# Edge counts from source ramps made on ScalarE beside VectorE's one-hots, with the first up-projection between the count batches

## The reference, cut to what matters

```python
e = jax.nn.leaky_relu(alpha_src[src] + alpha_dst[dst], NEG_SLOPE)
m = jax.ops.segment_max(e, dst, num_segments=n)
p = jnp.exp(e - m[dst])
denom = jax.ops.segment_sum(p, dst, num_segments=n)
out = jax.ops.segment_sum(h[src] * (p / denom[dst])[:, :, None], dst, num_segments=n)
```

## Time and profile before

| what | value |
|---|---|
| median of 3 runs | 1407.78 us (1406.85 to 1408.96) |
| the profiled execution's own time | 1407.49 us |
| its span, first to last instruction | 1405.7 us |
| TensorE busy | 1310.6 us, 93% |
| VectorE busy | 1004.6 us, 71% |
| ScalarE busy | 627.4 us, 45% |
| mean granted TensorE clock | 0.98 of 2.4 GHz |

### The profile page before, as it was taken

The page is one execution under the profiler, slowest core; times in us unless marked ns, Lnnn a source line. Parts: engine busy times, 40 slices in busy tenths (PEclk is TensorE's granted clock), DMA queues, the critical chain, the costliest instruction groups (busy, mean ns, idle before and its releaser), DMA issues.

```text
span 1405.7 us, 21373 instructions
## 1 busy us (share of the span) xinstructions
PE 1310.6 (93%) x7833; PEld 1149.2 (82%) x7833; DVE 1004.6 (71%) x1677; ACT 627.4 (45%) x795; POOL 217.0 (15%) x160
## 2 busy tenths in 40 slices
PE   5799999997899999997898999999999999999986
PEld 4499999974689999975777898898889888988875
DVE  7888888877797888875856765666566556656565
ACT  2256665644355666553434433433343334333431
POOL 0033444431024344431000000000000000002000
PEclk9999999998999999998999999999999999999988
DMA  9466556653256555653334454445444544543520
GB/s 346 147 202 198 164 164 180 213 134 93 91 196 199 180 164 164 192 160 113 113 111 152 163 198 170 149 166 199 158 149 177 195 149 149 188 177 134 177 69 23
DMA packets 103718, 227.32 MB, mean 162 GB/s; under 512 B 16688, under 2 KB 34672, under 8 KB 103684
## 3 DMA queue, kind: packets, MB, share of 16 engines
q1 hardware_dynamic: 72780, 192.43, 39.1%
q10 hardware_dynamic: 20968, 31.78, 7.7%
q0 software_dynamic: 9936, 2.66, 1.9%
HBM read 216.56 MB, written 10.29 MB: 161 GB/s over the span
## 4 chain that ended last, share of the span: by engine, by line
PE 61%; DVE 24%; issue 8%; ACT 4%; DMA 1%; DVEq 1%; ACTq 0%; SPq 0%
PE bank L418 59%; DVE w_lo L1181 6%; DVE hid_lo L1181 2%; DVE h_lo L1181 2%; DVE neg_b L1325 1%; ACT w_hi L892 1%; DVE scores_b L1276 1%; DVE stats L1219 1%; DVE scores_b L1278 1%; ACT z_b L960 1%; DMA w_in<-L_gnn_W 1%; DVE scores_b L1187 1%; PE bank L457 1%; DVE same L1299 1%; PE bank L514 1%
## 5 line engine op out<-in xcount | busy, mean ns | idle before, releaser
L1181 DVE TENSOR_TENSOR w_lo<-w_in,w_hi 128x2304 fp32r<-128x2304 f32 (+4 forms) x162 | 396.4, 2477 | 57.9 <-ACT w_hi L892 57.7
L892 ACT ACTIVATE w_hi<-w_in 128x2304 fp32r<-128x2304 f32 (+4 forms) x162 | 328.2, 2062 | 224.3 <-PE bank L418 197.2
L418 PE MATMUL bank<-w_hi,xT_hi 128*128 128x384 f32 (+3 forms) x942 | 324.1, 344 | 6.9 <-DVE xT_lo L1181 4.5
L418 PE MATMUL bank<-w_lo,xT_hi 128*128 128x384 f32 (+3 forms) x942 | 309.7, 341 | 0.0
L418 PE MATMUL bank<-w_hi,hid_hi 128*128 128x512 f32 (+2 forms) x858 | 293.9, 343 | 5.8 <-DVE hid_lo L1181 3.5
L418 PE MATMUL bank<-w_lo,hid_hi 128*128 128x512 f32 (+2 forms) x858 | 271.7, 337 | 0.0
L418 PE MATMUL bank<-w_hi,xT_lo 128*128 128x384 f32 (+3 forms) x942 | 248.0, 342 | 0.0
L418 PE MATMUL bank<-w_hi,hid_lo 128*128 128x512 f32 (+2 forms) x858 | 224.6, 339 | 0.0
L418 PEld LDWEIGHTS bank<-w_hi,xT_hi 128*128 128x128 f32 (+1 forms) x942 | 179.2, 190 | 36.4 <-issue 8.3
L418 PEld LDWEIGHTS bank<-w_hi,hid_hi 128*128 128x128 f32 (+1 forms) x858 | 161.7, 188 | 42.2 <-issue 5.3
L418 PEld LDWEIGHTS bank<-w_lo,xT_hi 128*128 128x128 f32 (+1 forms) x942 | 178.7, 190 | 13.7
(11 more groups left out here) (225 smaller groups left out, 1575.1 us busy)
## 6 DMA issues: line engine op xcount, KB each, us to landing
w_in<-L_gnn_W_rel SPq DMA_DIRECT2D x68, 1152.0 KB, 5.6
w_in<-L_gnn_W SPq DMA_DIRECT2D x66, 1152.0 KB, 5.8
table<-zrow SPq DMA_DIRECT2D x1, 9216.0 KB, 36.0
scores_b<-table ACTq DMA_DIRECT2D x34, 256.0 KB, 3.0
a_bc<-L_gnn_a_src ACTq DMA_DIRECT2D x18, 384.0 KB, 3.7
a_bc<-L_gnn_a_dst ACTq DMA_DIRECT2D x18, 384.0 KB, 5.0
key_row<-key_rows ACTq DMA_DIRECT2D x16, 256.0 KB, 5.5
w_in<-ffn_out SPq DMA_DIRECT2D x4, 864.0 KB, 7.2
```

The lines of the kernel that those rows point to most:

```text
L418: return pe.matmul(out, lhsT, rhs, start=start, stop=stop, **kw)
L892: act.activation(out, ps, func, **kw).then_inc(mark, 1)
L1181: return dve.tensor_tensor(out, a, b, op)
```

## The change

Every column but those of batch 0 now has its source row made in one of two places. The source row is no longer a one-hot but a ramp, max(0, i - src + 1) over the nodes i. ScalarE makes three of a batch's four (Relu with a bias per partition), VectorE the fourth; VectorE makes all four of batch 0. The counts are then the second differences of the sums along i, made once on VectorE. The key work, `low_tile` and the first batch's one-hots stand ahead of `low(1, 0)`; `biased(0)` moves to the end of the eight heads. On TensorE batches 1 to 9 stand one each behind k-steps 3, 4, 5 of tile 0 and 0 to 5 of tile 1, and batches 10 to 15 behind the last. `all_dst` moves from `a_bc` to `neg_b`, so a_src and a_dst are loaded before the count; the evictions of h and the four dot products stand between the batches. The second layer's count matrix and the clearing of `zt` come after the scores of head 0. SP waits for both halves of chunk 1 before it issues the clearing of the table. The 16 batches are written out rather than looped. `tile_dots` and `tile_low` are the old dots and `h_parts` under new names, and `keep_tile` is the old eviction of h; `cnt[.., 0]` gets its diagonal as before.

```diff
-        all_src, all_dst = batches(spare, N + REL), batches(a_bc[:, :, :].rearrange("p a n -> p (a n)"), N)
+        all_src, all_dst = batches(spare, N + REL), batches(flat_of(neg_b), N)
         hrow = prob[0:FH + 1, 0, :]
+        ramp_sum, ramp_step = alpha, spare[:, 0:M * (N + 2)].rearrange("p (m n) -> p m n", m=M)
+        ACT_RAMPS = G - 1
...
                     sp.wait_ge(zeroed, 1)
+                    for p in range(2):
+                        sp.wait_ge(w_full[p], 16)
                     sp.dma_start(table.rearrange("(p t) n -> p t n", p=P),
                                  zrow[:, :].unsqueeze(1).to_broadcast([P, ROWS // P, N])).then_inc(cleared, 16)
...
+                    def step_of(m, banks, k):
+                        if m == 0 and k % 3 == 0:
+                            pe.wait_ge(w_low[k // 3], n + 1)
+                        if first:
+                            of_tile(2 * layer, m)(k)
+                        return mm3([(bank[banks[j]][:, 0:HALF], part(w_hi, w_lo, slice(0, P), layer, k, slice(j * HALF, (j + 1) * HALF)))
+                                    for j in range(2)],
+                                   part(xT_hi, xT_lo, slice(0, P), k, slice(m * P, (m + 1) * P)), k == 0, k == K - 1)
+
+                    if first and between is not None:
+                        between(step_of)
+                        return
                     for m, banks in ((0, (5, 6)), (1, (3, 4))):
                         if not first:
 
                             pe.wait_ge(z_kept, (h + HEADS * layer) * 3 + (-2 if m == 0 else 0))
-                        if m == 1 and first:
-                            between()
...
+                spread(9 * layer)
                 if layer == 0:
                     pe.wait_ge(e_mask, 1)
+                    pe.wait_ge(e_kept, 2)
                 seed((0, 1, 2))
-                spread(9 * layer)
                 seed((0,) * 22)
                 turn(9 * layer)
                 seed((0,) * 5)
...
+            def count_batch(b):
+
+                pe.wait_ge(e_hot, b + 1)
+                if b:
+                    pe.wait_ge(e_ramp, b)
+                for g in range(G):
+                    for m in range(M):
+                        last = mm(bank[m][:, 0:N + REL], all_dst[:, b % RING, g, m * P:(m + 1) * P], all_src[:, b % RING, g, :],
+                                  False, False, skip_group_check=True)
+                last.then_inc(e_used, 1)
...
-                with pe.Fori(0, ET // G // RING) as i:
-                    for a in range(RING):
-                        count_batch(i * RING + a, a)
+                count_batch(0)
+                b = 1
+                for m, banks in ((0, (5, 6)), (1, (3, 4))):
+                    for k in range(K):
+                        last = step_of(m, banks, k)
+                        if k == K - 1:
+                            last.then_inc(*((h_mm, 1) if m == 0 else (w_used, 2)))
+                        if m or k > 2:
+                            count_batch(b)
+                            b += 1
+                for b in range(b, ET // G):
+                    count_batch(b)
...
-                    for m, banks in ((0, (5, 6)), (1, (3, 4))):
+                    for m in range(0 if layer or not first_head else M, M):
                         if m == 0:
                             act.wait_ge(h_mm, h + (HEADS * layer + 1))
                         else:
                             act.wait_ge(w_used, h * 2 + used(c0))
-                        for out, mark in ((h_sb, h_kept), (h_hi, h_high)):
-                            for j in range(2):
-                                keep(out[:, m, j * HALF:(j + 1) * HALF], bank[banks[j]][:, 0:HALF], mark)
+                        keep_tile(m, h_sb, h_kept)
+                        keep_tile(m, h_hi, h_high)
...
+            load_heads(0, 0)
             act.wait_ge(ld_const, 16 * 6)
             act.wait_ge(key_turned, 1)
             keep(key_t[:, :], bank[7][0:ET, 0:P], key_kept)
             act.wait_ge(key_kept, 1)
             act.dma_start(key_rows.rearrange("b (g n) -> (b g) n", g=G), key_t[:, :]).then_inc(key_put, 16)
+
+            act.wait_ge(consts, NCONST)
+            act.wait_ge(e_src, 1)
+            for b in range(1, ET // G):
+                act.wait_ge(e_used, b + 1)
+                for g in range(ACT_RAMPS):
+                    last = act.activation(all_src[:, b % RING, g, 0:N], iota[:, :], ACT.Relu, bias=edge_f[:, 0, b * G + g:b * G + g + 1])
+                last.then_inc(e_ramp, 1)
+                if b == 5:
+                    act.wait_ge(h_mm, 1)
+                    keep_tile(0, h_sb, h_kept)
+                    keep_tile(0, h_hi, h_high)
+                if b == 11:
+                    act.wait_ge(w_used, used(0))
+                    keep_tile(1, h_sb, h_kept)
+            keep_tile(1, h_hi, h_high)
+            act.wait_ge(e_cnt, 1)
+            keep(ramp_sum[:, 1, :], bank[1][:, 0:N], e_kept)
+            keep(rdeg[:, 1, :], bank[1][:, N:N + REL], e_kept)
             act.wait_ge(key_put, 16)
             act.dma_start(flat(key_row[:, :, :]), key_rows[0, :].partition_broadcast(P)).then_inc(ld_key, 16)
-            act.wait_ge(e_cnt, 1)
-            load_heads(0, 0)
             gat(0, lambda: load_heads(1, 0))
...
+            def scores(u, layer, ahead, together=False, begun=False, meanwhile=lambda: None):
+
+                if not begun:
+                    for m in range(M):
+                        tile_dots(u, m, junk[:, :], together)
+                    tile_low(u, 0, together)
...
-                h_parts(1)
+                tile_low(u, 1, together)
+                meanwhile()
...
+                if layer == 0:
+                    biased(0)
...
-            low_tile(0, 0)
-            low_tile(0, 1)
-            biased(0)
-            low(1, 0)
             dve.wait_ge(ld_edge, 48)
             step(dve.tensor_copy(edge_f[:, :, :], edge_i[:, :, :]))
             step(dve.scalar_tensor_tensor(key[:, :], edge_f[:, 2, :], float(N), edge_f[:, 0, :], mul, add_))
             dve.scalar_tensor_tensor(key[:, :], key[:, :], float(N), edge_f[:, 1, :], mul, add_).then_inc(key_made, 1)
+            low_tile(0, 0)
+            low_tile(0, 1)
+            ts(edge_f[:, 0, :], edge_f[:, 0, :], -1.0, mul, 1.0, add_).then_inc(e_src, 1)
             dve.wait_ge(key_made, 1)
+            dve.wait_ge(e_src, 1)
             step(ts(spill[:, :], key[:, :], -1.0, mul, pcol[:, 0:1], add_))
 
-            def one_hot(b, a):
+            def hot(b, ramps):
+                a = b % RING
                 dve.wait_ge(e_used, b + 1)
                 tt(all_src[:, a, :, N:N + REL], iota[:, 0:REL].unsqueeze(1).to_broadcast([P, G, REL]),
-                   edge_f[:, 2, bass.ds(b * G, G)].unsqueeze(2).to_broadcast([P, G, REL]), ALU.is_equal)
+                   edge_f[:, 2, b * G:(b + 1) * G].unsqueeze(2).to_broadcast([P, G, REL]), ALU.is_equal)
                 for g in range(G):
-                    for j, out in ((0, all_src[:, :, :, 0:N]), (1, all_dst)):
-                        last = dve.tensor_scalar(out[:, a, g, :], iota[:, :], edge_f[:, j, bass.ds(b * G + g, 1)], None, ALU.is_equal)
+                    last = dve.tensor_scalar(all_dst[:, a, g, :], iota[:, :], edge_f[:, 1, b * G + g:b * G + g + 1], None, ALU.is_equal)
+                for g in ramps:
+                    last = ts(all_src[:, a, g, 0:N], iota[:, :], edge_f[:, 0, b * G + g:b * G + g + 1], add_, 0.0, mx)
                 last.then_inc(e_hot, 1)
 
-            with dve.Fori(0, ET // G // RING) as i:
-                for a in range(RING):
-                    one_hot(i * RING + a, a)
-            for a in range(ET // G % RING):
-                one_hot(ET // G // RING * RING + a, a)
+            hot(0, range(G))
+            low(1, 0)
+            first_out = scores_b[:, :, :, :].rearrange("p a m n -> p (a m n)")[:, 0:D]
+            for b in range(1, ET // G):
+                hot(b, range(ACT_RAMPS, G))
+                if b == 7:
+                    tile_dots(0, 0, first_out)
+                    tile_low(0, 0)
+            tile_dots(0, 1, first_out)
+
             dve.wait_ge(e_cnt, 1)
-            for m in range(M):
-                for j in range(2):
-                    dve.tensor_copy(cnt[:, j, m, :], bank[m][:, 0:N])
-                last = dve.tensor_copy(rdeg[:, m, :], bank[m][:, N:N + REL])
-            step(last)
+            dve.tensor_copy(ramp_sum[:, 0, :], bank[0][:, 0:N])
+            dve.memset(ramp_step[:, :, 0:1], 0.0)
+            dve.tensor_copy(rdeg[:, 0, :], bank[0][:, N:N + REL]).then_inc(e_mask, 1)
+            dve.wait_ge(e_mask, 1)
+            dve.wait_ge(e_kept, 1)
+            dve.tensor_copy(ramp_step[:, :, 1:2], ramp_sum[:, :, 0:1])
+            step(tt(ramp_step[:, :, 2:N + 1], ramp_sum[:, :, 1:N], ramp_sum[:, :, 0:N - 1], ALU.subtract))
+
+            def counted(layer):
```

(11 more changed lines are left out.)

49 lines of the change are left out of this document (21 added, 28 removed).

## The result

The changed kernel takes **1400.18 us**, the median of five runs (1397.11 to 1400.92). The kernel before, run beside it, takes 1406.85 us (five runs, 1404.66 to 1408.96). The ratio is 0.9948 with a 95% interval of 0.9932 to 0.9964, so it is 6.7 us or 0.5% faster. The forecast was 1399.4 us within 1396.6 to 1403.5, with faster as the likeliest outcome.

The account below looks back on a forecast made before the run. Bound: TensorE, except in the count, where it waits for VectorE's one-hots. Scores -11.0 (start's 0.8 included), +1.3 given back, +1.5 clock: -8.2 us against 1407.49, 1399.3; forecast median 1399.4 us, range 1396.6 to 1403.5.

Parts of the forecast that it names:

- Rival (b): In the count, a maker becomes the bound (ramps at 0.51 or VectorE's slower form); 1.5 to 3.5 us back, 1402 us, chance 0.13.
- Rival (c): Weight chunk 2's first half lands at up to 54 us, moving ScalarE's exponential; 3 us, 1402.5 us, chance 0.05.
- Rival (d): In the count, late batches make k-steps hide nothing; 4.9 us go, 3 more with the clock down; 1407 us, chance 0.07.
- Rival (e): Slower: engines wait for code of the 16 written-out batches beside the clearing; two waits 11.4 us, 1411 us, chance 0.06.
- Start: Ahead of the up-projection: key work and batch 0 make TensorE begin at 19.9 instead of 19.07, 0.8 us lost.
- Scores: Head 0's scores on VectorE start at 52.2 instead of 63.19, 11.0 us won.
- The 4.9: Share of the 11.0 us won at the scores that the prediction gave to interleaving batches with k-steps on TensorE.
- Given back: Ahead of alpha, second matrix (0.69) and clearing (0.59) stand behind tile 1's remainder; 1.3 us given back.
- The clock: TensorE idle 3.7 us before alpha's transpose, clock 0.5 of 2.4 GHz behind it; 1.5 us lost.
- my case: The forecast itself, with TensorE's clock falling before alpha's transpose; -8.2 us, 1399.4 us, chance 0.48.
- rival (a): TensorE's clock does not fall behind the idle gap before alpha's transpose; -9.7 us, 1397.8 us, chance 0.21.
- the last sign that I named: The prediction is wrong if the shift at 76 us does not reach the end; later stages expected 8 us earlier.

Follow-up runs that it names:

- no_sp_wait: Changed kernel without SP's wait for both halves of chunk 1 ahead of the table's clearing; 1398.91 us, ratio 0.9931 to the kernel before.
- order_back: Changed kernel with TensorE's old order: node tile 0, all batches, closing matmuls, then node tile 1; 1399.47 us, ratio 0.9946 to the kernel before.
- second_later: Changed kernel with the second count matrix and the scratch tile's clearing moved behind the low part of chunk 2's second half; 1397.67 us, ratio 0.9922.
- after: The changed kernel's profiled execution in the result, the fastest of its five runs; 1397.11 us with a span of 1395.2 us.
- after_again: The changed kernel, unaltered, run and profiled a second time; 1398.70 us, ratio 0.9945 to the kernel before.
- after_third: The changed kernel, unaltered, run again as control of the runs with longer fills; 1398.68 us, ratio 0.9948 to the kernel before.
- ramps_dve: Changed kernel with all four ramps of a batch on VectorE and none on ScalarE; 1402.86 us, ratio 0.9962 to the kernel before.
- before: The profiled execution of the kernel before the change; span 1405.7 us.
- all_fill: Changed kernel with second matrix and clearing moved later, 32 fills for 22, and longer fills at nine further places; 1391.08 us, ratio 0.9891.
- dots_late: Changed kernel with the four dots and tile 0's remainder behind the diagonal instead of between batches; 1402.98 us, ratio 0.9960 to the kernel before.

## Why the prediction was right, and where it was not

**What it had right.** The mechanism: count matmuls bound by their maker, tile 1 and four dots standing in the same row, all of it movable beside TensorE's work. The closing matmuls came 0.1 us and the first copy 0.02 us from their forecast; ramps of 0.40 us (0.41), a batch on VectorE of 1.19 (1.2), and no slower form for two operations. Rival (b) is out, since both makers wait for TensorE and not the other way round. Rival (c) is out: chunk 2's half landed by 49.6, the wait of 1.00 us fits into slack, and no_sp_wait shows it by removal. Rival (d) is out, since batch and k-step follow each other at 2.07 us without a gap. Rival (e) is out, since no count matmul waits at all and no landmark up to the scores is more than 0.02 us later than forecast. Two slips of the prediction did no harm. It lets four batches stand alone where six do, seven with batch 9; the batches in store covered them, for no count matmul waited. And 1399.3 with the 0.3 for the median is 1399.6, not 1399.4.

**Start.** Forecast 19.9, measured 19.51, so the loss was 0.44 instead of 0.8 us. The key work ahead of xT_lo took the 0.8 us that I had put there (11.34 to 12.11) and delayed xT_lo by nothing, where I had allowed 0.1; what stands behind it took 0.49 us (14.63 to 15.12), where I had allowed 0.8.

**Scores.** Forecast -11.0, measured -11.7. The sum from the first copy to the scores was given as 4.0 us and was 3.29 (51.51 - 48.22). The 0.7 us are in the waits that I put between small operations: the rows show them starting one behind the other. The last wait of 0.3 is not there, and the rest is about 0.1 at each step (from the first copy to the column copy 0.57 for 0.7, the two subtractions 1.44 for 1.5).

**The attribution failed.** The step that fails is this sentence of the part on the scores: "Of that 4.9 come from the interleaving and 6.1 from dots, wait, remainder and copies no longer standing in the row." The 4.9 was the shift of the first copy, 53.05 to 48.2, and that shift is not what the interleaving does. order_back has the old order with the new makers, and its closing matmuls come at 43.2: the faster makers shift them by 9.2 us, and the interleaving then puts them 4.3 back and takes tile 1 out of the row in exchange, for a net of 2.2 us, some 1.5 without my placing. By removal, each from the whole change and so not made to add up: ScalarE's ramps are worth 5.3 us, the dots' place 4.8, the order 2.2 with the 0.66 of my placing in it. Three parts were not run apart, the move of `biased(0)`, the first batch ahead of `low(1, 0)` and the early load of a_src and a_dst, and no number here is theirs; nor was any other division of the four ramps than 3 to 1 and 0 to 4. Rival (d), priced at the same 4.9, was too dear for the same reason. The total held because it was worked out as the distance of two landmarks, which does not depend on how it is shared out afterwards.

**Given back.** The second matrix and the clearing: 1.3 us forecast, 1.42 by second_later.

**The clock.** Forecast: 3.7 us idle, 1.5 lost. Measured: 3.31 idle in all five executions that had the changed kernel's fill and chain, after, after_again, after_third, no_sp_wait and ramps_dve. By the way from transpose to last z_b it cost 1.16 in after, 1.19 in after_third, 0.37 in no_sp_wait (8.05 less 7.68), and nothing in after_again and ramps_dve. So my case and rival (a) were not two answers between which the trace decides. They are two outcomes of one kernel, and its median mixes them. Of the 1.5 the prediction's own rows gave 1.0 (0.4 and 0.6), and no row stood behind the other 0.5; where the clock fell fully it cost 1.2.

**From head 0 to the end.** Here the last sign that I named was only half met: the shift at 76 us should reach the end. It was 9.1 us, and 10.4 where the clock stayed (75.70 less 65.28). The medians show 6.7 us in the result, 7.8 and 7.3 beside after_again and after_third, the two pairs of profiled executions 10.5 and 10.8. The traces show where such differences arise. Taken at ScalarE's `high` of each weight half, which both traces have 162 times, the shift of after against before is 9.0 to 9.4 us through the heads of layer 0, 6.4 to 7.1 from 380 to 640 us, 8.1 at 700 us, 10.3 at 745 us, 8.9 from 774 to 1330 us, and 10.4 at 1355 us. It steps where layers and their parts meet, where one of the two executions has a stretch of low clock that the other lacks or has shorter. The execution of after_again does the same against after: 1.25 us ahead at 65 us, 1.8 to 3.0 ahead between 380 and 613, 1.2 behind at 735, 0.3 ahead from 765 us on. That is as large as what is asked for.

Which way it goes on average can be read from the granted clock of every execution, profiled or not. Its mean is 0.9783 over the 16 executions of the changed kernel (those of the result, of after_again and of after_third) and 0.9815 over 39 of the kernel before that ran beside the experiments. As time short of full clock, (1 - clock) x span, that is 30.3 and 26.0 us, 4.3 us apart with a standard error of 0.7. This is the most that it can have cost, since some of it falls on idle time, and head 0's own fall is in it. With the gaps filled the two kernels have the same clock (0.990), and there 12.0 us stand at the end for 11.5 in head 0. So the clock did fall more in the changed kernel, by an amount that is enough for the missing 2 to 3 us of the medians. That it accounts for them to the last part is argued, not shown. Why it falls more, why the same gap lets it fall in one execution and not in the next, and what spreads the runs of all_fill over 3.7 us stay open.

The forecast time, 0.8 us off the measured median, thus owes something to luck: head 0 gained 0.9 us more than forecast even where the clock fell (9.1 and 8.2), and the later stages passed on some 2 us less than all of it.

## What to carry to other kernels

Where a producer sets the pace of a ring and another engine is idle, give it part of the production even if it is slower per piece: 0.40 us against 0.197 for a ramp was worth 5.3 us at the scores here. A new order on the consumer is worth what its neighbours on other engines can start earlier, not the shift of its own last instruction; run the old order with the new makers to see which. When a chain gets shorter, resize the fills that covered it, and compare medians or landmarks ahead of the first stage with a varying clock; one pair of profiles (10.5 us here) can be off from the medians (6.7) by more than half of a gain of this size.

## What the runs showed of the hardware that was not expected

- Idle gaps of the same 3.31 us in TensorE were followed by a granted clock of 0.66 over 10 us in two executions, of 0.80 and 0.86 in a third, and of 1.00 in two others. The clock also fell at gaps of 1.91 us in second_later, of 2.10 us in order_back (0.50 from 52 to 55 us) and of 5.68 us in dots_late (0.50 from 52 to 57 us), and did not at the one of 1.17 us in the earlier trace rows.
- The clearing of the table took 31.4 us from issue to landing where SP waited for the first chunks, and 38.6 us in no_sp_wait, where it did not. The landing did not become a bound in either.
- Relu from a bf16 source with a bias for each partition starts every 0.40 us on ScalarE for 128x256, close to the 0.37 us of a Relu of f32 width, and it needed no table load ahead of it (the first ramp at 18.92 us had waited for a bank of TensorE).
